# Convolution images: two unstacked, one copy per 32 channels, padded by ScalarE

## What is computed

```python
x = x + _L0_conv_ref(_gn(x), L0_conv_W)
x = x + _L1_conv_ref(_gn(x), L1_conv_w_qkv, L1_conv_b_qkv, L1_conv_rpb, L1_conv_w_proj, L1_conv_b_proj)
```

## Time and profile before

| | |
|---|---|
| median of 3 runs | 1065.13 us (1064.41 to 1065.5) |
| the profiled execution, its own time | 1068.84 us |
| its span, first to last instruction | 1066.8 us |
| TensorE busy, of the span | 952.5 us (89%) |
| VectorE busy | 822.3 us (77%) |
| ScalarE busy | 642.4 us (60%) |
| GpSimd busy | 484.6 us (45%) |
| mean granted clock of TensorE | 0.87 |

### The profile page before, as it was taken

The page is one execution under the profiler, slowest core; times in us unless marked ns, Lnnn a source line. Parts: engine busy times, 40 slices in busy tenths (PEclk is TensorE's granted clock), DMA queues, the critical chain, the costliest instruction groups (busy, mean ns, idle before and its releaser), DMA issues.

```text
span 1066.8 us, 41868 instructions
## 1 busy us (share of the span) xinstructions
PE 952.5 (89%) x16669; PEld 630.3 (59%) x16669; DVE 822.3 (77%) x2117; ACT 642.4 (60%) x1808; POOL 484.6 (45%) x847
## 2 busy tenths in 40 slices
PE   4899997777899999999999999989999999999985
PEld 3455542235666666666676666656666666666763
DVE  4377876755879787887888787868897878788875
ACT  2111033205687868787777767666878686868653
POOL 7000002324474746464655555554647474646431
PEclk9755557678999989999899889998999898999997
DMA  9955555965555657474756465746665665737331
GB/s 233 218 161 134 136 135 148 285 185 172 165 152 167 192 142 202 118 227 103 215 144 203 117 191 143 209 118 186 163 180 155 166 186 147 205 99 226 104 87 39
DMA packets 131136, 175.00 MB, mean 164 GB/s; under 512 B 33624, under 2 KB 109944, under 8 KB 127616
## 3 DMA queue, kind: packets, MB, share of 16 engines
q1 hardware_dynamic: 125056, 157.94, 54.3%
q10 hardware_dynamic: 4608, 10.35, 3.8%
q0 software_dynamic: 1280, 4.05, 1.3%
HBM read 83.64 MB, written 67.55 MB: 142 GB/s over the span
## 4 chain that ended last, share of the span: by engine, by line
PE 64%; DVE 13%; issue 8%; ACT 7%; DMA 4%; ACTq 2%; SPq 2%; POOL 0%; DVEq 0%
PE PS L1453 14%; PE PS L1492 10%; PE PS L1476 8%; PE PS L1381 7%; PE PS L1398 6%; PE PS L1469 6%; PE PS L1435 5%; DVE area L1187 3%; DVE S L1208 3%; ACT area L845 3%; PE PS L1415 3%; ACT S L937 2%; DVE masked L1219 2%; PE PS L1502 2%; PE PS L1346 1%
## 5 line engine op out<-in xcount | busy, mean ns | idle before, releaser
L727 POOL TENSOR_TENSOR late<-masked 128x48 f32<-128x48 f32 (+1 forms) x512 | 152.6, 299 | 371.0 <-DVE masked L1219 359.7
L937 ACT ACTIVATE S<-S 128x384 f32<-128x384 f32 (+1 forms) x512 | 282.4, 554 | 25.2 <-DVE S L1208 21.8
L1208 DVE TENSOR_TENSOR S<-PS,bias 128x384 f32<-128x384 f32 (+1 forms) x512 | 282.4, 552 | 2.5 <-PE PS L1453 0.4
L1453 PE MATMUL PS<-area 97*128 97x48 bf16 (+1 forms) x4096 | 250.2, 208 | 37.9 <-DVE S L1208 32.7
L1198 DVE TENSOR_REDUCE mcol<-PS 128x6 bf16<-128x480 f32 (+2 forms) x288 | 176.1, 612 | 128.6 <-PE PS L1476 128.4
L930 ACT ACTIVATE VT<-PS 128x128 f32<-128x128 f32 x448 | 131.9, 294 | 182.6 <-PE PS L1435 179.2
L1453 PEld LDWEIGHTS PS<-area 97*128 97x128 bf16 x4096 | 179.0, 103 | 85.3 <-DVE S L1208 40.7
L1492 PE MATMUL PS<-S,VT 128*18 128x48 f32 x8192 | 197.0, 215 | 6.5 <-issue 5.9
L1492 PEld LDWEIGHTS PS<-S,VT 128*18 128x18 f32 x8192 | 117.4, 100 | 133.1 <-issue 66.2
L1476 PEld LDWEIGHTS PS<-area 128*128 128x128 bf16 x1568 | 144.9, 156 | 23.0 <-issue 8.7
L1435 PE MATMUL PS<-cst,area 128*128 128x128 f32 x448 | 141.9, 317 | 12.5 <-ACT VT L930 11.6
(11 more groups left out here) (102 smaller groups left out, 1017.9 us busy)
## 6 DMA issues: line engine op xcount, KB each, us to landing
area<-k_parts SPq DMA_DIRECT2D x32, 1008.0 KB, 7.1
area<-q_parts SPq DMA_DIRECT2D x64, 294.0 KB, 8.2
k_parts<-area SPq DMA_DIRECT2D x32, 504.0 KB, 8.1
k_parts<-area SPq DMA_DIRECT2D x32, 336.0 KB, 3.8
q_parts<-area SPq DMA_DIRECT2D x32, 294.0 KB, 7.3
area<-padded ACTq DMA_DIRECT2D x63, 112.2 KB, 3.9
out<-area SPq DMA_DIRECT2D x18, 392.0 KB, 4.1
late<-x_mid SPq DMA_DIRECT2D x17, 392.0 KB, 5.1
```

Of the source, the lines that this page charges most:

```text
L727: nc.gpsimd.tensor_tensor(sel[:, c % SEL_RING, :, :, t0:t0 + count], m[:, :, 0], m[:, :, 1], ALU.add).then_inc(s["summed"], 1)
L937: nc.scalar.activation(S[:, n % 4, 0:cols], S[:, n % 4, 0:cols], ACT.Exp).then_inc(s["probs"], 1)
L1208: nc.vector.tensor_tensor(S[:, n % 4, 0:cols], PS[:, SCORE + n % 2, 0:cols], bias[:, at:at + cols], ALU.add).then_inc(s["biased"], 1)
L1453: last = mm(PS[:, SCORE + n % 2, cols * g:cols * (g + 1)], key_rows[a][0:PEAK_ROW + 1, g, key:key + 128], query_rows[a][0:PEAK_ROW + 1, :, ...
```

## The change

Three things are done at once, with what they need around them.

- Images 0 and 1 are both convolved unstacked; images 2 to 15 are stacked.
- A stacked copy is one transfer per buffer of 32 channels: 96 partitions, channel by channel with its three shifts next to each other. So `wstack` is laid out anew (its rows by channel and shift, not by shift and channel) with a mask of its own. Up to image 12 SyncE and ScalarE issue two each; from image 13 on ScalarE issues all four.
- Images 2 to 15 are padded by ScalarE, as scale times value plus shift, in the slot's front, before it keeps the next input. VectorE computes the shift, minus mean times inverse deviation, in the four input chains.
- The product that makes `wconv` stands ahead of the first roots on VectorE; `wconv` is loaded in 4 transfers; the bias loads of ScalarE go to slots 5 to 11 and the weights' preparation to slot 13; `turn_patch` stands behind two rows of convolution.

```diff
-        def copy_image(eng, m, tiles):
+        def copy_tiles(eng, m, tiles):
+            if not stacked(m):
+                return
             eng.wait_ge(s["padded_ready"], m + 1)
-            if m > 2:
+            if m > FIRST_STACKED + 1:
                 eng.wait_ge(s["conv"], 2 * m - 2)
...
             for t in tiles:
-                for dc in range(3):
-                    eng.dma_start(copies(m)[t][32 * dc:32 * dc + 32, 0:SPAN], padded[m % 2][32 * t:32 * t + 32, dc:dc + SPAN]
-                                  ).then_inc(s[f"copies_in{m % 2}"], 16)
+                block_of = padded[m % 2][32 * t:32 * t + 32, 0:SPAN]
+                shifts = bass.AP(block_of.tensor, block_of.offset, [list(block_of.ap[0]), [1, 3], [1, SPAN]])
+                eng.dma_start(copies(m)[t][0:96, 0:SPAN], shifts).then_inc(s[f"copies_in{m % 2}"], 16)
...
+            def pad_image(m):
+                act.wait_ge(s["norm_ready"], m // X_RING + 1)
+                act.wait_ge(s["xin_kept"], 2 * m + 2)
+                act.wait_ge(s["conv"], 2 * m - 2)
+                small = smalls[0]
+                nc.scalar.activation(inner[m % 2], X[:, m, :].rearrange("p (r c) -> p r c", c=SIDE), ACT.Identity,
+                                     scale=small[:, RSTD, m:m + 1], bias=small[:, SHIFT, m:m + 1]).then_inc(s["padded_ready"], 1)
             for h in range(SLOTS):
                 for k in chain_at(h, 2):
                     root(k)
+                if h % 2 == 0 and PADS_BY_VECTOR <= h // 2 + 1 < IMAGES:
+                    pad_image(h // 2 + 1)
                 for side in range(2):
                     if TURN_FROM + h < IMAGES:
                         keep_input(TURN_FROM + h, side)
-                    if h % 2 == 0 and h // 2 + 1 < IMAGES:
-                        copy_image(act, h // 2 + 1, range(2 + side, 3 + side))
+                    if h % 2 == 0 and h // 2 + 1 < FIRST_BY_SCALAR:
+                        copy_tiles(act, h // 2 + 1, range(2 + side, 3 + side))
+                if h % 2 == 0 and FIRST_BY_SCALAR <= h // 2 + 1 < IMAGES:
+                    copy_tiles(act, h // 2 + 1, range(4))
...
+                if k in INPUT_CHAINS:
+                    link(nc.vector.tensor_scalar(small[:, SHIFT, :], small[:, MEAN, :], -1.0, None, ALU.mult))
+                    nc.vector.tensor_tensor(small[:, SHIFT, :], small[:, SHIFT, :], small[:, RSTD, :], ALU.mult
+                                            ).then_inc(s["norm_ready"], 1)
...
             spreads_of_groups(0)
+            dve.wait_ge(s["wconv_in"], 16 * NORM_GROUP)
+            nc.vector.tensor_tensor(wconv[:, :, :], wconv[:, :, :], group.unsqueeze(1).broadcast_to([128, 9, CH]), ALU.mult
+                                    ).then_inc(s["wconv_ready"], 1)
             inverse_roots(0)
             dve.wait_ge(s["cleared"], 4)
-            for i in range(2):
+            for i in range(PADS_BY_VECTOR):
                 pad_image(i)
...
                 if h % 2 == 0 and h:
-                    if h // 2 + 1 < IMAGES:
-                        pad_image(h // 2 + 1)
                     output_stats(h // 2 - 1)
...
-                if m:
+                if stacked(m):
                     for t in range(4):
```

85 lines of the change are left out of this document (47 added, 38 removed).

## The result

The changed kernel takes 1054.45 us, the median of 8 runs (1051.19 to 1064.46), the kernel before 1063.26 beside it (1058.66 to 1066.8). The ratio is 0.992, with a 95% interval of 0.9893 to 0.9948: faster by 8.8 us where 22.6 were forecast, near the upper edge of the range (1029 to 1057). A second comparison of the same two on another chip gave 1052.86 against 1064.58 (0.989, 0.9847 to 0.9932). The profiled execution took 1053.87, its span is 1052.0 us, the mean granted clock 0.886.

A forecast was written before the change was run, and what follows sets the result against it. It took TensorE at half clock to bound slots 4 to 16, with waits afterwards. Terms -0.8, -2, -8 and -11.8 sum to -22.6 from the profiled 1068.8, giving 1046.2; less 3.7 for the median, 1042.5 us, range 1029 to 1057.

The forecast's parts named there:

- slots 2 and 3: Early convolution: image 1 unstacked needs no copies, 15.1 us instead of 16.9; booked -2 us, bounds -1 and -3.
- In that gap the clock falls: Before slot 2, TensorE's 3.62 us wait for the second image's stacked copies was said to drop the clock to 0.50.
- Start: Path to the first convolution: one padded image and the weights' product leave it, about 1.1 us earlier; booked -0.8 (0 to -2).
- So I take nothing: Moving 16 bias loads off ScalarE's front: no gain, since ScalarE already waited for TensorE at the last of four images.
- Slots 4 to 16: Stacked convolution: full clock at slot 4, lost after about three slots taking some 16 us, not 23.6; -8 (0 to -19).
- Slots 17 to 31: Late convolution: less waiting for VectorE, ScalarE's issues and copies; together -11.8 us (-5 to -20).
- (a): Slots 17 on, up to 204.1 us: padding off VectorE, fewer ScalarE issues, patch transposes behind two convolution rows; -5 of 6.4 us.
- (c): Slot 28: nothing on SyncE stands before its copies, which are there by 215 us, before TensorE wants them; -5.3 us.
- Landings over 8 us: Sign against the forecast, which took 3.8 us for a merged copy to land, with 11.3 as upper end.
- The padded image: Padding on ScalarE: 0.9 us per image against 0.69 on VectorE, hidden; if cover is gone, 0.2 us per image.
- The clock holds: Rival: TensorE keeps the full clock through slot 16, -19 in place of -8, total 1031.5 us; chance 18%.
- The slower rival: Copies' round trip becomes the bound, with 96-row issues of 1.84 us and landings of 11.3: 1099 us; chance 5%.

The follow-up runs named there:

- the versions where the clock holds: One half of each image unstacked (images 2 to 8, 1 to 8 or 1 to 15), on the changed kernel with ScalarE keeping its input first: 1041.54, 1037.82, 1037.08 us.
- An edit of a few lines: Kernel before, with only the first half of every image from the second on unstacked: 1040.08 us, ratio 0.9795 to the kernel before.

## Why the prediction was half right

**Baseline: the step that failed.** The term "slots 2 and 3" and the sum were made against one execution, and all that was taken off for its being slower than the median was 3.7 us. "In that gap the clock falls" was true of that execution and of neither of the two others traced. In these the copies landed 2 us sooner, the clock survived, and slots 2 and 3 took 9.2 and 8.8 us instead of 16.9. Against them the term "slots 2 and 3", booked at -2 with bounds of -1 and -3, is +5.4 to +5.8, and the first stage gives -8.3. Nothing in the prediction bounded the case that the wait for the copies costs before only itself. Since the two other executions were fast ones, the median's share of this is less than the table's and not known. That "about 0.2%" could be told from no change was too hopeful as well: the intervals here are 0.3 to 0.5% to either side.

**Start.** Booked -0.8; the end of slot 1 came 3.6 us earlier. "So I take nothing" for the bias loads was the largest miss. The step looked at the last of the four input images alone. The chain of before runs through the loads' issues on ScalarE, then through all eight halves' statistics:

```profile
11.23 0.03 issue
11.26 0.61 ACTq L824
11.87 0.05 issue
11.91 0.90 ACT area L811 x2
12.83 3.87 DVE stats L1056 x8
```

ScalarE kept nothing before 11.9 us, and VectorE then had eight statistics to do in a row. Now three images are done when the last one's load lands at 12.24, and two statistics are left (14.37). The statistics end 1.3 us earlier (15.42 against 16.70); the path behind them to the convolution is 1.7 shorter, where 1.1 was taken, and the first two slots another 0.6. No run took these apart.

**Slots 2 and 3** were 14.6 us, with 15.1 forecast. Right for the changed kernel, wrong for what it replaces.

**Slots 4 to 16.** The clock fell at 62.1 in slot 6, where "after about three slots" put it, and slot 16 ended at 144.7, "near 144". The mechanism, TensorE ahead of VectorE and then waiting, was right for this trace. But the difference to before was -4.8, not -8, since slot 6 lost 3.1 us to waits (VectorE's bias 0.97, ScalarE's kept input 2.13), and -0.1 to -4.3 against executions that come to slot 4 at the full clock themselves.

**Slots 17 to 31.** Booked -11.8, measured -7.0 (-5.8 and -10.1 against the others). (a) The patches' wait went as said, by 6.6 us; putting the patches back moved most of the wait to the copies, and its median (1053.15 us) shows no difference. The padding's move accounts for about 5. (c) Slot 28's wait for copies went as said, and came back, 10.5 us long, with the copies on both queues. The landing is what was mis-sized: 5.9 us, where the row of equal size said 3.8, with late issues on ScalarE at some 1.2 us and not 0.6. It is the last of an image's four copies that TensorE waits for, and it is late twice over: in slots 26 and 30 it landed 11.9 and 11.0 us after the first of the four was issued (180.85 to 192.75, 206.72 to 217.68), where 2.4 + 3.8 = 6.2 was taken. So slots 22, 26 and 30 wait 9.4 us in all, where 4 to 6 were expected. Landings over 8 us, named as a sign of being wrong, are 4 of the 56. The row had the right bytes but not the right pattern: it was another copy, at another time.

**The padded image** on ScalarE cost 1.04 us (0.9 taken; the instruction has two pointer operands, scale and bias, where the estimate of 0.93 counted one) and was hidden, but for slot 6: what stood behind it was TensorE's input after all, when the root ahead of it was late.

**Attention** was costed at nothing. It took 827.7 us against 825.0, 825.2 and 820.8, and over all traced versions but the one wholly unstacked 820.8 to 828.6, without order. That it gives nothing is consistent with this; 3 us can't be excluded.

**The rivals.** "The clock holds" (1031.5) had a time near that of the versions where the clock holds (1037 to 1042), but by luck: they are other kernels, with more columns. In the changed kernel it fell at 62.1. The slower rival needed landings of 10 us; they were 5.9 in the median, with 8.6 the longest.

## What to carry to other kernels

Before a wait is priced, look at several executions of the same kernel: a wait at the edge of a clock change can be worth 1.6 us or, with the work behind it at half the clock, 9 (3.62 and 5.7), and the trace at hand shows one of the two. A form of the work that needs a third of the columns was no faster here, since its slots ran at half the clock. A mixture of both forms beat the stacked one by 14 us or more and the unstacked one by some 48; which half of an image was unstacked made no difference (ratios 0.98 and 0.9812). An edit of a few lines was worth about twice the whole change; look first at the granted clock of each stretch and at what runs in it.

## Unexpected of the hardware

- The clock did not return in 66.8 us of uninterrupted stacked convolution, transposes and selections, in any execution that lost it before slot 8. It returned within 3.4 us where unstacked matmuls were among them, and once within 3.4 us in stacked records alone (219.3 to 222.7).
- It survived waits of 1.2 and 1.6 us at the head of slot 2 and fell in one of 3.6; in slot 6 of the changed kernel it fell behind one of 0.97.
- A copy to 96 partitions landed 5.9 us after its issue (median, 3.6 to 8.6), copies of a third of it 3.1. Behind stores of `q_parts` on SyncE one took 12.76.
- Executions of the kernel before differ by 14 us within one comparison (1054.3 to 1068.8). One cause is seen in the traces: the clock is lost at 42.4, 52.7 or 67.1 us.
